# Two-layer sequence model on one core: norm scalars, a folded MLP bias and shifted write vectors take other engines, in another order

## What is computed

```python
xn = layernorm(x)
# layer 0
m = mamba_block(xn)          # in_proj, conv, selective scan (512 channels, 16 states), gate, out_proj
f = gelu(m @ ffn_w1.T + ffn_b1) @ ffn_w2.T + ffn_b2
c = m + f
x = x + (c - mean(c)) / sqrt(var(c) + EPS) + experts(xn)   # mean and var over the whole sequence
xn = layernorm(x)
# layer 1
seq_out = causal_attention(xn @ qkv_w + qkv_b)             # 16 heads of 16
x_prev = concatenate([zeros, xn[:, :-1]], axis=1)
w1, w2 = x_prev @ w1_write, xn @ w2_write
write_lines = exterior(w1, w2)                             # 6 products w1_i w2_j - w1_j w2_i, normalized
...                                                        # decayed sum of squared incidences, gated
x = x + (seq_out + gated * mem_val) @ out_w + out_b + mlp(xn)
```

## Time and profile before

| | us |
|---|---|
| median of 3 runs (lowest, highest) | 3748.41 (3742.24, 3749.98) |
| the profiled execution's own time | 3745.62 |
| its span in the trace | 3743.9 |

### The profile page before, as it was taken

The page is one execution under the profiler, slowest core; times in us unless marked ns, Lnnn a source line. Parts: engine busy times, 40 slices in busy tenths (PEclk is TensorE's granted clock), DMA queues, the critical chain, the costliest instruction groups (busy, mean ns, idle before and its releaser), DMA issues.

```text
span 3743.9 us, 63558 instructions
## 1 busy us (share of the span) xinstructions
PE 3543.0 (95%) x20512; PEld 2364.9 (63%) x20512; DVE 3169.1 (85%) x6019; ACT 2654.0 (71%) x4087; POOL 2278.8 (61%) x1790
## 2 busy tenths in 40 slices
PE   7999999999999999999888999999999999999998
PEld 3666666656556665656665766767676676767665
DVE  3798999999999999999977688786968778696873
ACT  5878878788787878888634757566675757667565
POOL 3797999999999999999934142332514233251421
PEclk9999999999999999999898999999999999999999
DMA  4445445554554555545532123232312323231220
GB/s 155 134 162 166 161 148 181 155 170 163 167 167 148 177 166 166 170 149 178 191 97 97 42 78 101 70 109 70 115 48 81 98 70 115 64 122 48 75 84 21
DMA packets 253340, 456.88 MB, mean 122 GB/s; under 512 B 26116, under 2 KB 80852, under 8 KB 250196
## 3 DMA queue, kind: packets, MB, share of 16 engines
q1 hardware_dynamic: 253012, 452.82, 38.7%
HBM read 381.07 MB, written 69.21 MB: 120 GB/s over the span
## 4 chain that ended last, share of the span: by engine, by line
PE 50%; DVE 22%; issue 10%; ACT 8%; POOL 7%; DMA 2%; DVEq 0%; SPq 0%; POOLq 0%; ACTq 0%
DVE ps L2071 8%; PE ps L1661 6%; PE ps L1548 5%; PE ps L1653 5%; PE ps L1529 4%; POOL drive L2326 4%; PE ps L1511 3%; DVE heavy L2049 3%; ACT ps L1678 3%; PE ps L1413 3%; DVE held L2071 3%; PE ps L1463 2%; PE ps L1380 2%; ACT L1678 2%; PE ps L1588 2%
## 5 line engine op out<-in xcount | busy, mean ns | idle before, releaser
L2326 POOL TENSOR_TENSOR drive<-du,b_wide 128x1024 f32<-128x1024 f32 x512 | 1202.6, 2366 | 147.7 <-DVE held L2071 80.1
L1678 ACT ACTIVATE ps<-delta,neg_a 128x512 f32<-128x512 f32 x1024 | 684.4, 686 | 184.4 <-DVE heavy L2049 115.7
L1678 ACT ACTIVATE exps<-ps 128x1024 f32<-128x1024 f32 (+1 forms) x640 | 599.7, 939 | 228.9 <-PE ps L1529 224.9
L2360 POOL TENSOR_SCALAR_AFFINE_SELECT exps<-exps 128x256 f32<-128x256 f32 x512 | 204.4, 414 | 832.5 <-ACT exps L1678 832.5
L2094 DVE CUSTOM_DVE_ANT_0 ps<-ps,later 128x512 f32<-128x512 f32 (+3 forms) x1024 | 474.6, 518 | 55.1 <-PE ps L1511 53.1
L2049 DVE TENSOR_TENSOR heavy<-c_wide,ps 128x512 f32<-128x512 f32 x704 | 450.5, 676 | 15.2 <-issue 14.1
L1463 PEld LDWEIGHTS ps<-p_all,heavy 128*128 128x128 f32 x3072 | 355.2, 142 | 152.5 <-issue 76.9
L2071 DVE TENSOR_TENSOR_SCAN ps<-ps,carry,drive 128x512 f32<-128x512 f32 x352 | 434.8, 1274 | 10.6 <-ACT ps L1678 10.6
L1463 PE MATMUL ps<-p_all,heavy 128*128 128x128 f32 x3072 | 415.0, 277 | 23.3 <-DVE heavy L2049 20.8
L2071 DVE TENSOR_TENSOR_SCAN ps<-ps,drive 128x512 f32<-128x512 f32 x352 | 414.0, 1215 | 25.3 <-ACT ps L1678 21.9
L2310 POOL TENSOR_TENSOR held<-held,c_wide 128x1024 f32<-128x1024 f32 x160 | 378.4, 2365 | 6.4
(11 more groups left out here) (212 smaller groups left out, 7175.2 us busy)
## 6 DMA issues: line engine op xcount, KB each, us to landing
b_wide<-bc_dram SPq DMA_DIRECT2D x512, 256.0 KB, 3.4
c_wide<-bc_dram SPq DMA_DIRECT2D x512, 256.0 KB, 3.6
stacks<-parts SPq DMA_DIRECT2D x192, 256.0 KB, 2.5
qs<-stacks SPq DMA_DIRECT2D x128, 192.0 KB
ks<-stacks SPq DMA_DIRECT2D x128, 192.0 KB, 4.4
x_row<-in_x SPq DMA_DIRECT2D x14, 1024.0 KB, 7.9
resid<-mix SPq DMA_DIRECT2D x9, 1024.0 KB, 5.5
x_row<-resid SPq DMA_DIRECT2D x9, 1024.0 KB, 6.1
```

The source lines that it names most:

```text
L1678: return nc.scalar.activation(out_, in_, func, **kw)
L2326: G.tensor_tensor(drive[:, g % DRIVE_SLOTS, :, :], du[:, e, :, :], wide(b_wide[:, g % B_SLOTS, :], MD), ALU.mult).then_inc(driven, 1)
```

## The change

- **Norm scalars.** `offset` goes from VectorE to GpSimd. `square` and `shift` become one ScalarE instruction each (Identity with scale and bias, Copy with scale).
- **Second MLP bias.** `fb2` is transposed once into a column per block (`bias`), and ScalarE adds it to `mT` when it empties the bank. `o` then carries it through its transposes. As `mT` feeds the first product too, `fix` subtracts `W1 * fb2` from the bias `fb1`, once. `o` is a plain copy by ScalarE; `centre` waits for it.
- **Gate.** One instruction of 1,024 columns in place of four of 256.
- **Write vectors.** `pb` is six matmuls of 320 columns from unshifted tokens; ScalarE writes the 64 columns to a new buffer `ahead` (one slot per tile, slot 0 zero). Per half sequence, SyncE moves them to `pt1` one partition down in two transfers (`shift`); the four outer products of the half wait for them. The zero columns of `xT` are no longer written.
- **Order.** `SHIFTS` has other numbers for most kinds, and `STAY` is 0.02 (was 0.03); the planner's tasks follow the changes above.

```diff
-                    for one in xT:
-                        V.memset(one[:, :, 0:1].bitcast(F32), 0.0).then_inc(setup1_v, 1)
...
-                elif kind == "offset":
-                    dve.wait_ge(scale_done, parts_done(b, part))
...
-                    V.tensor_tensor(ln_shift[:, own], ln_minus[:, own], ln_rstd[:, own], ALU.mult).then_inc(offset_done, 1)
+                if kind == "offset":
+                    own = tiles_of(j, i)
+                    pool.wait_ge(scale_done, parts_done(j, i))
+                    pool.wait_ge(minus_done, parts_done(j, i))
+                    pool.wait_ge(norm_done, NT * j)
+                    G.tensor_tensor(ln_shift[:, own], ln_minus[:, own], ln_rstd[:, own], ALU.mult).then_inc(offset_done, 1)
...
+                elif kind == "square":
+                    act.wait_ge(row_apart, j + 1)
+                    f(row_q[:, 1:2], row_q[:, 4:5], ACT.Identity, scale=row_q[:, 4:5], bias=row_mv[:, 1:2]).then_inc(row_square, 1)
+                elif kind == "shift":
+                    drained(act, L0_PLAN, ("mu", j), "v")
+                    act.wait_ge(row_inverse, j + 1)
+                    f(row_q[:, 2:3], row_q[:, 0:1], ACT.Copy, scale=row_q[:, 3:4]).then_inc(row_shift, 1)
...
-                    V.tensor_tensor(mix[:, t, :], bank[:, 0:D], param("fb2"), ALU.add).then_inc(drained_v, 1)
+                elif kind == "fix":
+                    V.tensor_tensor(param("fb1"), param("fb1"), full(dve, L0_PLAN, task)[:, 0:MF], ALU.subtract).then_inc(drained_v, 1)
...
+                elif kind == "o":
+                    t = TC * (j % NC) + unit[2]
+                    if unit[2] == 0 and j % NC == 0:
+                        act.wait_ge(x0_stored, 16)
+                        if j:
+                            act.wait_ge(x_kept, 16 * (j // NC))
+                    f(mix[:, t, :], bank[:, 0:D], ACT.Copy).then_inc(drained_a, 1)
...
-                    f(mT[:, unit[2], :], bank, ACT.Copy).then_inc(drained_a, 1)
+                    f(mT[:, unit[2], :], bank, ACT.Identity, bias=late_bias[:, unit[2]:unit[2] + 1]).then_inc(drained_a, 1)
...
+                elif kind == "bias":
+                    pe.wait_ge(params_more_in, 16)
+                    for k in range(KD):
+                        last = tp(bank[:, k * P:(k + 1) * P], param("fb2")[:, k * P:(k + 1) * P], ident)
+                elif kind == "fix":
+                    drained(pe, L0_PLAN, ("bias", 0), "a")
+                    pe.wait_ge(mlp0_up_in, 16)
+                    for m in range(MF):
+                        for k in range(KD):
+                            last = mm(bank[:, m:m + 1], w_up0[:, k, m * P:(m + 1) * P], late_bias[:, k:k + 1],
+                                      start=(k == 0), stop=(k == KD - 1))
...
-                for t in range(TC):
-                    part = of_pair(gate[j % 2][:, t, :], e)
-                    V.tensor_tensor(part, acc_tile(t), part, ALU.mult).then_inc(y_gated, 1)
+                part = gate[j % 2][:, :, e * MD * P:(e + 1) * MD * P]
+                V.tensor_tensor(part, ps[:, 0:2, :].rearrange("p b (h d) -> p (b h) d", h=2), part, ALU.mult)\
+                    .then_inc(y_gated, TC)
...
+                        last = mm(bank[:, 0:D + 64], xT[of][:, k, tokens(t)], w[by][:, k, :], start=(n == 0),
+                                  stop=(n == len(three) - 1))
...
+                    f(ahead[:, task[2] + 1, :], bank[:, D:D + 64], ACT.Copy).then_inc(drained_a, 1)
...
+                elif kind == "shift":
+                    c = task[2]
+                    drained(sp, plan, ("pb", n, TC * c + TC - 1), "a")
+                    sp.wait_ge(ahead_set, n + 1)
+                    if NC * n + c:
+                        sp.wait_ge(outer_done, TC * (NC * n + c))
+                    sp.dma_start(pt1[1:P, :, 0:64], ahead[0:P - 1, TC * c + 1:TC * (c + 1) + 1, :]).then_inc(shifted, 16)
+                    sp.dma_start(pt1[0:1, :, 0:64], ahead[P - 1:P, TC * c:TC * (c + 1), :]).then_inc(shifted, 16)
...
                 elif kind == "outer":
                     t = task[2]
                     drained(pool, plan, ("pb", n, t), "a")
+                    pool.wait_ge(shifted, 32 * (NC * n + t // TC + 1))
```

More of the change, by code:

```diff
@@ L101, in prelude_units @@
     return ([("xt", 0, 0, k) for k in range(KD)] + [("xm", 0, m) for m in range(MI)] + [("cv", 0, m) for m in range(MI)]
-            + [("res", 0, t) for t in range(2)] + [("xd", 0)] + [("dl", 0, m) for m in range(MI)])
+            + [("res", 0, t) for t in range(2)] + [("bias", 0), ("xd", 0)] + [("dl", 0, m) for m in range(MI)])
 NH = B * NC
@@ L570, in layer1_tasks @@
                       ("v", "gate", b - 1, NC - 1) if b else None, ("p", "zt", b - 2, NC - 1, KD - 1) if b > 1 else None,
-                      a=[("g", "outer", (n - TC) // NT, (n - TC) % NT)] if n >= TC else [])
-                dense(("pb", b, t), ("p", "pa", b, t))
-                add("g", ("outer", b, t), 1.05, place["pb", b, t], ("a", "pb", b, t),
+                      a=([("g", "outer", (n - TC) // NT, (n - TC) % NT)] if n >= TC else []) + ([("s", "shift", b - 1, NC - 1)] if b and t == 0 else []))
+                dense(("pb", b, t), ("p", "pa", b, t), a=[("s", "shift", b - 1, NC - 1)] if b else [])
+                if t % TC == TC - 1:
+                    add("s", ("shift", b, c), 0.8, place["pb", b, t], ("a", "pb", b, t),
+                        ("g", "outer", (n - TC) // NT, (n - TC) % NT) if n >= TC else None, late=2.2)
+            for t in range(TC * c, TC * (c + 1)):
+                n = NT * b + t
+                add("g", ("outer", b, t), 1.05, place["pb", b, t], ("s", "shift", b, c),
                     ("v", "lines", (n - 2) // NT, (n - 2) % NT) if n >= 2 else None)
@@ L656 @@
 TURN, DRIFT = 0.1, 0.042
-SHORT, RUN, STAY = 0, 1, 0.03
+SHORT, RUN, STAY = 0, 2, 0.02
 PULL = {"a": 0.016, "v": 0, "g": 0, "s": 0.0}
 SHIFTS = {
[3 rows of a table removed]
-    ("g", 0): {"drive": 6, "weigh": 5, "du": 13, "join": 4.8},
[6 rows of a table removed]
-    ("v", 0): {"scan": 43, "weigh": -39, "stats": 14.4},
-    ("v", 1): {"gate": 42, "wo": -12, "bias": 34, "mt": 6, "sm": 1.9, "ot": -22, "xt": 18, "lines": 14, "normal": 19},
+    ("a", 0): {"xt": -23, "res": 21, "skip": 18, "decay": 2.9, "gelu": 20, "soft": 25, "root": 36, "norm": 3.6,
+        "xd": -54, "mh": 3, "m": -2, "xm": -7, "gelu_t": 24, "shift": -20, "yt": 1.5, "dl": -3, "h": -5, "o": -0.7},
+    ("a", 1): {"logistic": 82, "length": 74, "f1": -21, "qk": 39, "gelu": 18},
+    ("g", 0): {"drive": 5.6, "join": -5, "weigh": -7},
+    ("g", 1): {"feat_w": -46, "outer": -47, "sum": 15},
[6 rows of a table added]
+    ("v", 0): {"scan": 49, "spreads": 24, "mo": 18, "scale": 49, "gate": 6},
+    ("v", 1): {"gate": 64, "pb": 13, "sm": 5, "mt": 39, "ms": 16, "unit": 37, "bias": 39, "split": -9, "pa": 18,
+        "wo": 5, "zeros": 18, "qk": 2},
 }
@@ L931, in build @@
         zero_rows = rows[80:82, 0, :]
[L933 to L934 removed]
+        pt1, pt2, ahead, outer, lines, norm, feat_w, feat_r, gsum, lines_at = place(
+            body_at, ("pt1", [P, TC, 2 * 4 * H]), ("pt2", [P, TC, 2 * 4 * H]), ("ahead", [P, NT + 1, 64]), ("outer", [P, 2, 2 * H, 4, 4]),
             ("lines", [P, 2, TC, 2 * H, 6]), ("norm", [P, TC * 2 * H]), ("feat_w", [P, TC, NPQ * H]),
@@ L2314, in _ @@
             G.memset(const[:, 1:2], float(H)).then_inc(consts_set, 1)
+            for part in range(NC):
+                row_task(("offset", 0, part))
             row_task(("du", 0, 0))
```

102 lines of the change are left out of this document (45 added, 57 removed), and 15 rows, old and new, of the table SHIFTS.

## The result

The changed kernel takes **3,823.82 us** (median of four runs, 3,818.35 to 3,827.56) against 3,746.45 us before (four runs, 3,742.24 to 3,749.98): a ratio of **1.0206**, 95% interval 1.0188 to 1.0224. It is 2.1% slower, where 1.7% faster was forecast. The profiled execution has a span of 3,820.6 us.

What follows compares the result with a forecast made beforehand. VectorE, closely followed by GpSimd and TensorE, was taken to bound the scan stage, TensorE the second. -43 - 25 + 4 + 1 = -63 us against 3,745.62 gave 3,682.6, as a median 3,685 us; range 3,640 to 3,728.

Steps and rivals of the forecast that it cites:

- The transfers: Second stage, write vectors moved by SyncE: landing 2.5 us, last outer product 5.8 us later, costed at nothing more.
- Rival 4: Second stage: late line vectors stall TensorE at the features' transposes, up to 16 x 5.8 = 93 us, 3,778 us; chance 0.07.
- The cover named: Second stage: GpSimd busy only 494.68 of 1,450 us, and TensorE has a sequence of attention to put between.
- The new order: All queues: reordering by other offsets could move 17 us either way near the seams; taken as zero.
- The scan stage: 400 to 1,902 us: VectorE's work falls 3.7 us per half, 3.2 us counted as gain over 13.4 halves, 43 us.
- the folded bias: Before the scans: transposes and eviction in the prelude cost 1 us, sixteen one-column products with a stall 4 us.
- rival 2: Scan stage: output evictions on ScalarE's queue delay TensorE and decays, nothing comes back there, 3,728 us; chance 0.10.
- The tiny instructions: Scan stage, norm scalars: two on ScalarE and one on GpSimd per sequence, some 0.2 to 0.3 us each.
- the eviction of 0.47 us: Scan stage, MLP output: ScalarE gets four evictions of 128x256 per half, 470 ns by the nearest row, 1.9 us.
- The write vectors' work on TensorE: Second stage: six products of 320 columns at 0.147 us replace twelve, saving 25 us (ends 10 and 33).
- rival 3: Second stage: TensorE is not the bound, work saved on pb turns into idle time, 3,710 us; chance 0.10.

Runs made afterwards that it cites:

- the quick transfer: Changed kernel with the 127 rows sent as 112 and 15, 3,739.06 us; with the second stage's offsets of the kernel before as well, 3,843.69 us.

## Why the prediction was wrong

- **The transfers: the step that failed.** The prediction bounded the landing by 2.5 us, from a transfer of 256 KB, and costed the step at nothing. Measured: 9.8 us from issue to first use, and 7 us during which SyncE's queue was held. The nearest row was near in kind but not in shape: it showed no transfer of 127 rows. The kernels lie 77 us apart; one cut gives back 85 to 87.
- **Costing the step at nothing fails near the prediction's own landing, too.** With the cut the rows are used 3.5 us after the first issue, 1 us later than the prediction had it, and still 53 of the 139 us by which the second stage missed the forecast (114 longer instead of 25 shorter) are there. Four outer products that come late together, and an order searched for them, changed at once; no run parts the two, so this rest stays open.
- **Rival 4 had the cause, but neither the place nor the size** (16 halves, up to 5.8 us each, 3,778 us). The line vectors were late in each half, but TensorE did not stand at the transposes of the features: it waited for `feat_w` once, 2.9 us in the whole run, and in the attention for 92 us from 2,150 to 3,600 us (the three rows of waits in the section on the result). Its price came from the same 2.5 us; with 9.8 in its place it is 16 x (9.8 + 3.3) = 210 us at most, where 139 were missing. It was given 0.07 because TensorE waited only 0.9 us for that chain before. That row told how well the old order hid a chain that followed tile by tile, not how much a new one could bear. The cover named (a sequence of attention between) was not there: the attention's own exponentials, masks and maxima stood behind the outer products on ScalarE, GpSimd and VectorE.
- **The clock was missing from the rival's price.** Of the 127 us lost from 1,910 to 3,600 us, 81 are idle time and some 46 the lower clock while TensorE worked.
- **The new order, taken as zero within 17 us**, is no separate term, and the bound was far too narrow. It goes with the write vectors: new offsets without them cost 57 us (3,797 against 3,740), old offsets with them 105 us even with the quick transfer.
- **The scan stage was right**: 108.8 us per half against 108.9, 37.5 us sooner against 43 less 5 for the folded bias. VectorE's waits for ScalarE's decays before scans fell from 17.7 to 11.8 us, so rival 2 fell; those for GpSimd's drive grew (16.9 us in 9.19 halves, 1.8 us per half), as GpSimd is now as full as VectorE. The tiny instructions fell as forecast; the eviction of 0.47 us took 0.37.
- **The write vectors' work on TensorE was right**: six products of 320 columns start 0.145 us apart with the cut (0.147 forecast; the second and the last of one unit below), 96 products fewer in two sequences, and work at full clock down by 22 us in eight, near the 25 forecast. That the time follows is not shown: in no run did a sequence get shorter by it, so rival 3 (the saved work turns into idle time) is neither refuted nor, as order and outer products changed with it, borne out.

```profile
2363.42 0.31 PE L1625 MATMUL ps<-w_hi,xT_lo 128*128 128x320 f32 x1
...
2364.00 0.31 PE L1625 MATMUL ps<-w_lo,xT_hi 128*128 128x320 f32 x1
```

- **One reading of the rows was wrong, without harm to the sum.** The prediction took L2013's 0.15 us as against the lock-out by GpSimd's products. VectorE's timeline before (first fence) beside GpSimd's (second):

```profile
750.40 0.15 DVE L2013 TENSOR_TENSOR row_q<-row_q 128x1 f32<-128x1 f32 x1
750.59 2.20 DVE L2015 TENSOR_TENSOR row_q<-row_q,row_mv 128x1 f32<-128x1 f32 x1
```

```profile
748.11 2.36 POOL L2310 TENSOR_TENSOR held<-held,c_wide 128x1024 f32<-128x1024 f32 x1
750.44 2.33 POOL L2326 TENSOR_TENSOR drive<-du,b_wide 128x1024 f32<-128x1024 f32 x1
```

L2013 starts as one product ends (within 0.1 us), L2015 0.15 us into the next, and ends with it. All five of each in the even stretch lie so. How long the instruction takes depends on where in GpSimd's product it starts, and L2013 is no exception.

## What to carry to other kernels

Price a new transfer by its own shape, first the count of its slowest dimension: cut 127 rows into 112 and 15. When work that went out one by one becomes a batch at the end, its whole chain is late at once: look at what else stands in those queues, and count the clock after the hole with the hole. An order searched together with a change cannot be judged apart from it: undoing either half alone left it slower (3,797 and 3,942 us) than undoing both (3,740).

## What was not expected of the hardware

- 127 rows of 1 KB moved between partitions at 18 to 25 GB/s in one transfer, 112 of them at up to 283 GB/s; the two issues of 112 and 15 rows took 1.6 to 1.7 us together in most halves.
- 508 pieces of 256 bytes behind one issue held the next transfer on SyncE's queue for 6.8 to 7.1 us; 127 pieces of 1 KB, 0.6 to 1.4 us. 448 pieces of 256 bytes as 112 rows did not.
- Two slices of 5 us in which TensorE was busy 0.61 and 2.03 us came with some 10 us at the lower clock (0.76, 0.50 and 0.72 in three slices), the last of it with TensorE busy throughout. From 1,910 to 3,600 us this cost some 46 us beside 81 us of holes.
